# Graph attention with LayerNorm: k and q weights staged by column pieces, first scores after two projections, v's low parts on GpSimd

## The chip, the core and the metric

The kernel runs on one NeuronCore of a Trainium2 chip. A core has five engines with instruction streams of their own: TensorE (PE in the profile), VectorE (DVE), ScalarE (ACT), GpSimd (POOL) and SyncE (SP, used here for DMA issues only). They meet through semaphores. The metric is the device time of one execution in microseconds (us), as the median of several executions.

## The reference, cut to what matters

```python
# x: (128 graphs, 128 nodes, 512); adj: (128, 128, 128); 16 heads of 32
q = split_heads(x @ Wq.T)
k = split_heads(x @ Wk.T)
v = split_heads(x @ Wv.T)
bias = (adj + adj)[:, None]
a = jnp.einsum('bhnd,bhmd->bhnm', q, k) * scale + bias
row_nonzero = jnp.any(a != 0, axis=-1, keepdims=True)
a = jnp.where(row_nonzero, a, -jnp.inf)
p = jax.nn.softmax(a, axis=-1)
p = jnp.where(jnp.isnan(p), 0.0, p)
o = jnp.einsum('bhnm,bhmd->bhnd', p, v)
o = o.transpose(0, 2, 1, 3).reshape(B, N, D)
y = _layernorm(x + o @ Wo.T)
```

## The kernel before

Four graphs make a group (512 nodes), so there are 32 groups. The 512 channels are cut into 4 chunks of 128 for the contraction and 4 head tiles of 128 columns (4 heads) for the output. One phase is one head tile of one group: 128 phases. `scores(f)` makes the scores of phase f in PSUM. VectorE then adds the doubled adjacency and takes row maxima (`bias`, line 851), takes row minima (`smallest`, 859), forms row factors (`largest`, `any_nonzero`, `row_factors`, lines 866, 874, 891), scales the exponentials (`normalise`, 897) and turns them in blocks of 32 (`turn_blocks`, 907), in two halves of two graphs each. ScalarE makes the exponentials (`exps`, line 699) between the two, and copies every finished projection out of PSUM (`take`). SyncE carries the turned blocks through DRAM (`save_blocks`, `move_blocks`), and two phases later `values(f)` multiplies them with v.

A projection is called a product here: (kind, tile or graph, groups ahead). A product is done at fp32 precision as three matmuls of parts for each chunk, 12 matmuls of 128x512: every operand is split into a high part (a rounded copy, on ScalarE) and a low part (the rest, a subtraction of two SBUF tensors). The helper `rest` on VectorE is line 780, and on GpSimd line 349. Which products stand between two `scores` is written out by hand in `BEFORE`, `FIRST_PLAN` (group 0), `PLAN` and `LAST_PLAN`. The three PSUM banks of products are used in the order of these lists, and `take` follows them.

```python
FIRST_PLAN = [[("q", 1, 0), ("v", 0, 0), ("v", 1, 0), ("v", 2, 0)],
              [("k", 2, 0), ("q", 2, 0), ("v", 3, 0), ("v", 0, 1)],
              [("k", 3, 0), ("q", 3, 0), ("v", 1, 1)],
              [("k", 0, 1), ("q", 0, 1), ("v", 2, 1)]]
BEFORE = [("k", 0, 0), ("q", 0, 0), ("k", 1, 0)]
```

At the start, ScalarE's queue loads the k weights and SyncE's queue loads everything else, in chunks of 256 KB (128 partitions of 2 KB): xt of group 0, q, v, adjacency, xt of group 1, o. They land in tiles that the phases will use later (`w_stage`, `xt_stage`). VectorE makes the low parts of xt of group 0 and of k, q and v. GpSimd makes those of xt of group 1 and of o. Before phase f+1's `scores`, TensorE waits for ScalarE's copies of k and q (`k_copied`, `q_copied`) and for VectorE's `bias` of phase f.

The functions that the change touches, with the profile's line numbers:

Of the kernel before, what the change touches and what calls it, by code (L numbers as in the profile page):

```python
# [42 lines left out]
FIRST_PLAN = [[("q", 1, 0), ("v", 0, 0), ("v", 1, 0), ("v", 2, 0)],  # L43
# [7 lines left out]
BEFORE = [("k", 0, 0), ("q", 0, 0), ("k", 1, 0)]  # L51
# [60 lines left out]
def build(nc, xt_d, x_d, adj_d, wq_d, wk_d, wv_d, wo_d, out_d, blocks_d):  # L112
    ctx = ExitStack()
    with ctx:  # L114
# [6 lines left out]
        def sem(name):  # L121
# [101 lines left out]
        w_stage = {"k": v_sb[:, 1], "q": e_sb[:, :].rearrange("p a b c -> p a (b c)"),  # L223
                   "v": v_sb[:, 0], "o": x_sb[:, :, :]}
# [19 lines left out]
        def _(sp):  # L244
            def stage_w(kind, c):
                sp.dma_start(w_stage[kind][:, c], {"q": wq_d, "v": wv_d, "o": wo_d}[kind][:, c]
                             ).then_inc(w_loaded[kind, c], 16)

# [85 lines left out]
        def _(pool):  # L334
# [121 lines left out]
        def _(pe):  # L456
# [46 lines left out]
            def first_product(kind, index):  # L503
                def early(c):
                    pe.wait_ge(xt_hi_done, c + 1)
                    pe.wait_ge(w_hi_done, c + 1)

                def before(c):
                    if kind == "k":
                        pe.wait_ge(xt0_lo_done, c + 1)  # L510
                    n = CH * ORDER.index(kind) + c + 1
                    pe.wait_ge(w_hi_done, n)
                    pe.wait_ge(w_lo_done, n)
                weight_product(kind, 0, index, before if index == 0 else None, early if kind == "k" else None)
# [69 lines left out]
            for f in range(LAST):  # L584
# [3 lines left out]
                for kind, g, index in slots(f):  # L588
                    if g == 0 and kind == "v":
# [44 lines left out]
        def _(act):  # L634
# [107 lines left out]
            take(-1, 2)
            for f in range(PHASES):
# [3 lines left out]
                if f == 0:  # L747
                    act.wait_ge(w_lo_done, 2 * CH)
# [6 lines left out]
                if f == 0:  # L755
                    weight_hi("o")
# [21 lines left out]
        def _(dve):  # L778
# [3 lines left out]
            def weight_lo(kind, c):  # L782
                dve.wait_ge(w_hi_done, CH * ORDER.index(kind) + c + 1)
                w = WEIGHT[kind]
                rest(w_lo[:, w, c, :], w_stage[kind][:, c], w_hi[:, w, c, :]).then_inc(w_lo_done, 1)
# [131 lines left out]
            for c in range(CH):  # L917
                weight_lo("v", c)
# [73 lines left out]
```

## Time and profile before

| what | value |
|---|---|
| median of 3 executions | 1736.4 us (1736.4 to 1737.27) |
| profiled execution, its own time | 1735.29 us |
| its span in the profile | 1733.5 us |
| TensorE busy | 1708.4 us |
| VectorE busy | 1589.5 us |
| ScalarE busy | 1368.2 us |
| GpSimd busy | 962.1 us |

The profiled execution took 1735.29 us by its own time, 1.8 us of which lie outside the span. Its time is 1.1 us below the median of the three. The program has 128 phases, so one phase is some 13.3 us in the steady part.

### The profile page before, as it was taken

The numbers are of one execution on the slowest core, as the hardware profiler recorded it, in microseconds if no ns is written. First come the engines' busy times: TensorE is split into PE (matmuls) and PEld (weight loads), VectorE is DVE, ScalarE is ACT, GpSimd is POOL, SyncE is SP. The second block draws the span as 40 slices with busy tenths as digits, with TensorE's granted clock in tenths as the row PEclk, the third lists the DMA queues.
The fourth block names the chain that finished last, engine by engine and source line by source line (L and its number), as shares of the span: only waits on it lengthen the run. The fifth ranks groups of instructions, "written<-read, shape, count | busy, mean of one in ns | idle before, by whom it ended". The sixth has DMA issues, their size and how long they took to land. (4 is left out here: it accounts for less than half of the span.)

```text
span 1733.5 us, 45700 instructions
## 1 busy us (share of the span) xinstructions
PE 1708.4 (99%) x14370; PEld 1379.8 (80%) x14370; DVE 1589.5 (92%) x5815; ACT 1368.2 (79%) x5134; POOL 962.1 (55%) x1516
## 2 busy tenths in 40 slices
PE   9899999999999999999999999999999999999996
PEld 7788888888888888888888888788888888888884
DVE  7999999999999999999999999999999999999996
ACT  7787788788778877887788788778877887888775
POOL 2255556555555555565555555555655556556543
PEclk9999999999999999999999999999999999999999
DMA  6677777777777777777777777777777777777764
GB/s 213 199 225 216 226 225 227 223 216 230 226 220 225 232 218 226 214 233 224 215 231 228 223 229 215 223 225 224 234 220 216 225 225 227 226 211 234 211 200 168
DMA packets 275378, 382.59 MB, mean 221 GB/s; under 512 B 25152, under 2 KB 155200, under 8 KB 275008
## 3 DMA queue, kind: packets, MB, share of 16 engines
q1 hardware_dynamic: 274560, 378.64, 74.1%
q8 instruction: 113, 1.85, 0.5%
q14 instruction: 129, 1.06, 0.2%
q10 hardware_dynamic: 576, 1.05, 0.2%
HBM read 212.86 MB, written 166.72 MB: 219 GB/s over the span
## 5 line engine op out<-in xcount | busy, mean ns | idle before, releaser
L699 ACT ACTIVATE e_sb<-neg_a,neg_max 128x128 f32<-128x128 f32 x2048 | 793.2, 391 | 164.2 <-DVE neg_max L851 164.2
L851 DVE CUSTOM_DVE_ANT_0 neg_a<-ps_s,adj_sb 128x128 f32<-128x128 f32 x2048 | 442.4, 286 | 67.3 <-PE ps_s L536 67.1
L469 PE MATMUL ps_w<-xt_hi,w_lo 128*128 128x512 f32 x1020 | 414.4, 406 | 0.0
L470 PE MATMUL ps_w<-xt_lo,w_hi 128*128 128x512 f32 x1020 | 400.4, 393 | 0.0
L699 ACT ACTIVATION_READ_ACCUMULATOR e_sb<-neg_a,neg_max 128x1 f32 x2048 | 387.9, 189 | 0.0
L907 DVE STREAM_TRANSPOSE e_b<-e_sb 128x1024 f32<-128x1024 f32 x254 | 316.3, 1245 | 27.2 <-DVE e_sb L897 0.9
L349 POOL TENSOR_TENSOR o_lo<-o_sb,o_hi 128x512 fp32r<-128x512 f32 x126 | 163.8, 1300 | 289.7 <-ACT o_sb L636 289.7
L897 DVE SCALAR_TENSOR_TENSOR e_sb<-e_sb,r_inv 128x1024 f32<-128x1024 f32 x256 | 316.4, 1236 | 8.1 <-DVE r_inv L891 0.5
L859 DVE TENSOR_REDUCE neg_min<-neg_a 128x16 f32<-128x2048 f32 x128 | 292.6, 2286 | 4.4
L472 PE MATMUL ps_w<-xt_hi,w_hi 128*128 128x512 f32 x1020 | 274.0, 391 | 0.0
L469 PEld LDWEIGHTS ps_w<-xt_hi,w_lo 128*128 128x128 f32 x1020 | 191.3, 188 | 64.5 <-issue 25.3
L365 POOL TENSOR_TENSOR x_sb<-y_sb,x_sb 128x512 f32<-128x512 f32 x122 | 156.5, 1283 | 145.0 <-ACT y_sb L636 144.8
L472 PEld LDWEIGHTS ps_w<-xt_hi,w_hi 128*128 128x128 f32 x1020 | 191.7, 188 | 42.1
L470 PEld LDWEIGHTS ps_w<-xt_lo,w_hi 128*128 128x128 f32 x1020 | 191.9, 188 | 36.8
L636 ACT ACTIVATE y_sb<-ps_w 128x512 f32<-128x512 f32 x122 | 72.8, 597 | 165.7 <-PE ps_w L472 165.7
L469 PE MATMUL ps_w<-w_hi,xt_lo 128*128 128x512 f32 x512 | 199.4, 389 | 0.0
L470 PE MATMUL ps_w<-w_lo,xt_hi 128*128 128x512 f32 x512 | 199.3, 389 | 0.0
L469 PE MATMUL ps_w<-w_hi,o_lo 128*128 128x512 f32 x496 | 193.3, 390 | 0.0
L470 PE MATMUL ps_w<-w_lo,o_hi 128*128 128x512 f32 x496 | 193.1, 389 | 0.0
L851 DVE DVE_READ_ACCUMULATOR2_ANT neg_max<- 128x1 f32 x2048 | 170.5, 83 | 0.0
L536 PEld LDWEIGHTS ps_s<-k_sb,q_sb 32*128 32x128 f32 x4096 | 126.0, 186 | 52.2 <-issue 52.2
L349 POOL TENSOR_TENSOR xt_lo<-xt_raw,xt_hi 128x512 fp32r<-128x512 f32 x120 | 158.2, 1319 | 15.8 <-ACT xt_hi L636 15.8
(104 smaller groups left out, 2622.4 us busy)
## 6 DMA issues: line engine op xcount, KB each, us to landing
blocks<-e_b SPq DMA_DIRECT2D x1016, 128.0 KB, 2.2
e_t<-blocks SPq DMA_DIRECT2D x127, 1024.0 KB, 7.2
x_sb<-x SPq DMA_DIRECT2D x124, 256.0 KB, 4.8
out<-x_sb SPq DMA_DIRECT2D x124, 256.0 KB, 3.6
xt_raw<-xt SPq DMA_DIRECT2D x120, 256.0 KB, 4.8
adj_sb<-adj SPq DMA_DIRECT2D x32, 256.0 KB, 5.1
v_sb<-wk ACTq DMA_DIRECT2D x4, 256.0 KB, 6.4
neg_a<-xt SPq DMA_DIRECT2D x4, 256.0 KB, 5.9
```

Of the source, the lines that this page charges most:

```text
L349: return pool.tensor_tensor(out, whole, hi.bitcast(F32), ALU.subtract)
L365: pool.tensor_tensor(row, y_sb[:, :], row, ALU.add).then_inc(added, 1)
L469: pe.matmul(out, lhs_lo(c), rhs_hi(c), start=(c == 0), stop=False)
L470: pe.matmul(out, lhs_hi(c), rhs_lo(c), start=False, stop=False)
L472: last = pe.matmul(out, lhs_hi(c), rhs_hi(c), start=False, stop=(c == chunks - 1))
L536: last = pe.matmul(ps_s[h][:, nodes], q_sb[rows, slot, nodes], k_sb[rows, slot, nodes], start=True, stop=True)
L636: return act.activation(out, in_, ACT.Copy, scale=scale)
L699: last = act.activation(e_sb[:, i, h, :], neg_a[:, i, h, :], ACT.Exp, scale=-1.0, bias=neg_max[:, i, h:h + 1], accum_out=sums[:, i, h:h + 1])
L851: last = dve.tensor_tensor_reduce(out=neg_a[:, i, h, :], in0=ps_s[h][:, i * NODES:(i + 1) * NODES], in1=adj_sb[:, g % PAIR, i, :], scale=- ...
L859: dve.tensor_reduce(neg_min[:, :].rearrange("p a b -> p (a b)"), neg_a[:, :].rearrange("p a b c -> p (a b) c"), AX.X, ALU.max).then_inc(mi ...
L897: dve.scalar_tensor_tensor(out=e_sb[:, two].rearrange("p i h n -> p (i h) n"), in0=e_sb[:, two].rearrange("p i h n -> p (i h) n"), scalar=BIG,
L907: dve.transpose(blocks[:, half], e_sb[:, 2 * half:2 * half + 2].rearrange("p i h (b j) -> p (i h) b j", b=BLOCKS)).then_inc(transposed, 1)
```

## The change

The staged weights of k and q are cut by columns of the output instead of by chunks of the contraction. `PIECES` gives three pieces: the columns of head tile 0, those of head tile 1, and those of tiles 2 and 3 together. A piece holds all four chunks, so the first piece of k is all that the first product needs of k. The first pieces of k and q are loaded on ScalarE's queue, the other four on SyncE's. The high parts of the six pieces are on ScalarE. The low parts of the four narrow pieces are on VectorE, and those of the two wide ones on GpSimd (two instructions of 128x1024 elements). The low parts of v (four of 128x512) move from VectorE to GpSimd. q is staged in `x_sb` instead of `e_sb`, so ScalarE's wait before the first exponentials goes, and SyncE now waits for all pieces of k and q to be split before it loads o. The high parts of xt of group 1 move behind the exponentials of phase 0, those of o behind phase 1's.

```diff
-FIRST_PLAN = [[("q", 1, 0), ("v", 0, 0), ("v", 1, 0), ("v", 2, 0)],
-              [("k", 2, 0), ("q", 2, 0), ("v", 3, 0), ("v", 0, 1)],
-              [("k", 3, 0), ("q", 3, 0), ("v", 1, 1)],
+FIRST_PLAN = [[("k", 1, 0), ("q", 1, 0), ("v", 0, 0), ("v", 1, 0)],
+              [("k", 2, 0), ("q", 2, 0), ("v", 2, 0), ("v", 3, 0)],
+              [("k", 3, 0), ("q", 3, 0), ("v", 0, 1), ("v", 1, 1)],
-BEFORE = [("k", 0, 0), ("q", 0, 0), ("k", 1, 0)]
+BEFORE = [("k", 0, 0), ("q", 0, 0)]
+PIECES = [slice(0, P), slice(P, 2 * P), slice(2 * P, D)]
...
+            def stage_piece(kind, n):
+                cols = PIECES[n]
+                sp.dma_start(w_stage[kind][:, :, cols], {"k": wk_d, "q": wq_d}[kind][:, :, cols]
+                             ).then_inc(piece_loaded[kind, n], 16)
...
-            for c in range(CH):
-                stage_w("q", c)
+            stage_piece("k", 1)
+            stage_piece("q", 1)
             for c in range(CH):
                 stage_w("v", c)
             sp.dma_start(adj_sb[:, 0], adj_d[0]).then_inc(adj_loaded[0], 16)
+            stage_piece("k", 2)
+            stage_piece("q", 2)
             for c in range(CH):
                 stage_chunk(1, c)
+            sp.wait_ge(piece_hi_done, 6)
+            sp.wait_ge(piece_lo_done, 4)
+            sp.wait_ge(rest_lo_done, 2)
             for c in range(CH):
                 stage_w("o", c)
...
             for c in range(CH):
+                pool.wait_ge(wv_hi_done, c + 1)
+                rest(w_lo[:, WEIGHT["v"], c, :], w_stage["v"][:, c], w_hi[:, WEIGHT["v"], c, :]).then_inc(wv_lo_done, 1)
+            for kind in "kq":
+                w, cols = WEIGHT[kind], PIECES[2]
+                pool.wait_ge(piece_hi_done, 5 + "kq".index(kind))
+                rest(w_lo[:, w, :, cols], w_stage[kind][:, :, cols], w_hi[:, w, :, cols]).then_inc(rest_lo_done, 1)
...
+            def piece_hi(kind, n):
+                act.wait_ge(piece_loaded[kind, n], 16)
+                copy(w_hi[:, WEIGHT[kind], :, PIECES[n]], w_stage[kind][:, :, PIECES[n]]).then_inc(piece_hi_done, 1)
...
+            piece_hi("k", 0)
             for c in range(CH):
                 staged_hi(0, c)
-                act.wait_ge(w_loaded["k", c], 16)
-                copy(w_hi[:, WEIGHT["k"], c, :], w_stage["k"][:, c]).then_inc(w_hi_done, 1)
-            weight_hi("q")
+            piece_hi("q", 0)
             take(-1, 0)
+            piece_hi("k", 1)
+            piece_hi("q", 1)
+            take(-1, 1)
             weight_hi("v")
-            take(-1, 1)
-            for c in range(CH):
-                staged_hi(1, c)
-            take(-1, 2)
...
+                    if f == 0 and i == 1:
+                        piece_hi("k", 2)
+                        piece_hi("q", 2)
...
+            piece_lo("k", 0)
             for c in range(CH):
                 dve.wait_ge(xt_hi_done, c + 1)
                 rest(xt_lo[:, 0, c, :], xt_stage[0, c], xt_hi[:, 0, c, :]).then_inc(xt0_lo_done, 1)
-                weight_lo("k", c)
-            for c in range(CH):
-                weight_lo("q", c)
-            for c in range(CH):
-                weight_lo("v", c)
+            piece_lo("q", 0)
+            piece_lo("k", 1)
+            piece_lo("q", 1)
```

The first place is ScalarE at the start of the program, before. `v_sb` stages k here, `neg_a` stages xt of group 0.

```order
L731 DMA v_sb<-wk 128x512 x4
L636 ACT_TABLE_LOAD
L636 ACTIVATE xt_hi<-neg_a 128x512 [waits xt_staged00]
L636 ACTIVATE w_hi<-v_sb 128x512 [waits wk_loaded0]
L636 ACTIVATE xt_hi<-neg_a 128x512 [waits xt_staged01]
L636 ACTIVATE w_hi<-v_sb 128x512 [waits wk_loaded1]
```

The same place of the changed kernel, up to the copy of the first q product; `x_sb` stages q.

```order
L773 DMA v_sb<-wk 128x4x128
L773 DMA x_sb<-wq 128x4x128
L673 ACT_TABLE_LOAD
L673 ACTIVATE w_hi<-v_sb 128x4x128 [waits k_piece_loaded0]
L673 ACTIVATE xt_hi<-neg_a 128x512 [waits xt_staged00]
L673 ACTIVATE xt_hi<-neg_a 128x512 [waits xt_staged01]
L673 ACTIVATE xt_hi<-neg_a 128x512 [waits xt_staged02]
L673 ACTIVATE xt_hi<-neg_a 128x512 [waits xt_staged03]
L673 ACTIVATE w_hi<-x_sb 128x4x128 [waits q_piece_loaded0]
L673 ACTIVATE k_sb<-ps_w 128x512 [waits k_made]
L673 ACTIVATE w_hi<-v_sb 128x4x128 [waits k_piece_loaded1]
L673 ACTIVATE w_hi<-x_sb 128x4x128 [waits q_piece_loaded1]
```

Eight conversions and the four of q before the first copy out of PSUM have become six, and the one that all others stand behind waits for the first piece of k.

The second place is GpSimd from its first real work on, before.

```order
L349 TENSOR_TENSOR xt_lo<-e_t,xt_hi 128x512 [waits xt_hi_done,consts]
L349 TENSOR_TENSOR xt_lo<-e_t,xt_hi 128x512 [waits xt_hi_done] x3
L349 TENSOR_TENSOR w_lo<-x_sb,w_hi 128x512 [waits w_hi_done] x4
L349 TENSOR_TENSOR o_lo<-o_sb,o_hi 128x512 [waits values_copied]
L349 TENSOR_TENSOR xt_lo<-xt_raw,xt_hi 128x512 [waits xt_hi_done] x2
```

The same place of the changed kernel. The first two rows are v's, the next two k's and q's wide pieces, then xt of group 1 and o.

```order
L365 TENSOR_TENSOR w_lo<-v_sb,w_hi 128x512 [waits wv_hi_done,consts]
L365 TENSOR_TENSOR w_lo<-v_sb,w_hi 128x512 [waits wv_hi_done] x3
L365 TENSOR_TENSOR w_lo<-v_sb,w_hi 128x4x256 [waits piece_hi_done]
L365 TENSOR_TENSOR w_lo<-x_sb,w_hi 128x4x256 [waits piece_hi_done]
L365 TENSOR_TENSOR xt_lo<-e_t,xt_hi 128x512 [waits xt_hi_done] x4
L365 TENSOR_TENSOR w_lo<-x_sb,w_hi 128x512 [waits wo_hi_done] x4
L365 TENSOR_TENSOR o_lo<-o_sb,o_hi 128x512 [waits values_copied]
```

Six subtractions, two of them twice as wide, now stand ahead of the eight that were there.

The third place is ScalarE in phase 0, before.

```order
L699 ACTIVATE e_sb,sums<-neg_a,neg_max 128x128 [waits biased]
L699 ACTIVATE e_sb,sums<-neg_a,neg_max 128x128 x3
L636 ACTIVATE q_sb<-ps_w 128x512 [waits q_made]
L699 ACTIVATE e_sb,sums<-neg_a,neg_max 128x128 [waits biased]
L699 ACTIVATE e_sb,sums<-neg_a,neg_max 128x128 x3
```

The same place of the changed kernel, and on to the end of the phase.

```order
L673 ACTIVATE k_sb<-ps_w 128x512 [waits k_made]
L673 ACTIVATE w_hi<-v_sb 128x4x256 [waits k_piece_loaded2]
L673 ACTIVATE w_hi<-x_sb 128x4x256 [waits q_piece_loaded2]
L741 ACTIVATE e_sb,sums<-neg_a,neg_max 128x128 [waits biased]
L741 ACTIVATE e_sb,sums<-neg_a,neg_max 128x128 x3
L741 ACTIVATE e_sb,sums<-neg_a,neg_max 128x128 [waits biased]
L741 ACTIVATE e_sb,sums<-neg_a,neg_max 128x128 x3
L673 ACTIVATE q_sb<-ps_w 128x512 [waits q_made]
L673 ACTIVATE xt_hi<-e_t 128x512 [waits xt_staged10]
L673 ACTIVATE xt_hi<-e_t 128x512 [waits xt_staged11]
```

Between the exponentials of the phase's two halves stand two conversions of 128x1024, and the four of xt of group 1 come behind the second half.

## Rows read from the trace of the kernel before

**Rows 1.** The page, part 1: busy time (share of the span), instructions.

```profile
PE 1708.4 (99%) x14370; PEld 1379.8 (80%) x14370; DVE 1589.5 (92%) x5815; ACT 1368.2 (79%) x5134; POOL 962.1 (55%) x1516
```

**Rows 2.** Busy by stretch: stretch, us, busy of each engine (instructions), PEclk, DMA, GB/s.

```profile
140.00:200.00 60.00, 60.00 (x517) 48.56 (x519) 55.18 (x192) 47.21 (x178) 35.24 (x58) 1.00 0.76 225
200.00:1700.00 1500.00, 1496.18 (x12671) 1210.92 (x12663) 1392.12 (x5136) 1197.32 (x4521) 864.06 (x1352) 1.00 0.76 223
```

**Rows 3.** Waits of TensorE: line, waited for: us in total, times, longest.

```profile
PE ps_s L536 <- issue: 7.0, 5, 2.0
```

**Rows 4.** Timeline, TensorE, the scores (L536): start us, us, [idle before].

```profile
18.24 1.17 PE L536 MATMUL ps_s<-k_sb,q_sb 32*128 32x128 f32 x32
...
54.82 1.17 PE L536 MATMUL ps_s<-k_sb,q_sb 32*128 32x128 f32 x32 [1.56 <-issue]
...
66.97 1.17 PE L536 MATMUL ps_s<-k_sb,q_sb 32*128 32x128 f32 x32 [1.58 <-issue]
...
79.28 1.17 PE L536 MATMUL ps_s<-k_sb,q_sb 32*128 32x128 f32 x32 [1.75 <-issue]
...
92.50 1.17 PE L536 MATMUL ps_s<-k_sb,q_sb 32*128 32x128 f32 x32
```

**Rows 5.** Timeline, VectorE, the first bias instruction of phases 0 to 3.

```profile
19.59 0.29 DVE L851 CUSTOM_DVE_ANT_0 neg_a<-ps_s,adj_sb 128x128 f32<-128x128 f32 x1 [2.65 <-PE ps_s L536]
...
33.27 0.25 DVE L851 CUSTOM_DVE_ANT_0 neg_a<-ps_s,adj_sb 128x128 f32<-128x128 f32 x1
...
45.38 0.25 DVE L851 CUSTOM_DVE_ANT_0 neg_a<-ps_s,adj_sb 128x128 f32<-128x128 f32 x1
...
57.48 0.25 DVE L851 CUSTOM_DVE_ANT_0 neg_a<-ps_s,adj_sb 128x128 f32<-128x128 f32 x1
```

**Rows 6.** Timeline, VectorE, scaling and row factors of phase 0's two halves.

```profile
26.09 1.23 DVE L897 SCALAR_TENSOR_TENSOR e_sb<-e_sb,r_inv 128x1024 f32<-128x1024 f32 x1
...
28.72 1.06 DVE L891 SCALAR_TENSOR_TENSOR r_inv<-recip,nonzero 128x8 f32<-128x8 f32 x1
29.81 2.26 DVE L897 SCALAR_TENSOR_TENSOR e_sb<-e_sb,r_inv 128x1024 f32<-128x1024 f32 x1
```

**Rows 7.** Timeline, GpSimd, its two trains of subtractions in the first 40 us.

```profile
17.28 5.02 POOL L349 TENSOR_TENSOR xt_lo<-e_t,xt_hi 128x512 fp32r<-128x512 f32 x4 [15.51 <-ACT xt_hi L636]
28.46 6.03 POOL L349 TENSOR_TENSOR w_lo<-x_sb,w_hi 128x512 fp32r<-128x512 f32 x4 [6.15 <-ACT w_hi L636]
```

**Rows 8.** Timeline, ScalarE: first conversions, then phase 0's exponentials and copies.

```profile
5.12 0.63 ACT L636 ACTIVATE xt_hi<-neg_a 128x512 fp32r<-128x512 f32 x1 [1.22 <-DMA neg_a<-xt]
5.66 0.61 ACT L636 ACTIVATE w_hi<-v_sb 128x512 fp32r<-128x512 f32 x1
...
20.62 0.40 ACT L699 ACTIVATE e_sb<-neg_a,neg_max 128x128 f32<-128x128 f32 x1 [0.97 <-DVE neg_max L851]
...
23.72 0.57 ACT L636 ACTIVATE q_sb<-ps_w 128x512 f32<-128x512 f32 x1
...
27.28 0.57 ACT L636 ACTIVATE v_sb<-ps_w 128x512 f32<-128x512 f32 x1
```

**Rows 9.** Timeline, TensorE, product matmuls: the first ones, then two products' first.

```profile
6.42 0.77 PE L461 MATMUL ps_w<-xt_hi,w_hi 128*128 128x512 f32 x1 [0.39 <-ACT w_hi L636]
...
7.79 0.63 PE L464 MATMUL ps_w<-xt_lo,w_hi 128*128 128x512 f32 x1
8.21 0.63 PE L461 MATMUL ps_w<-xt_hi,w_hi 128*128 128x512 f32 x1
...
22.19 0.39 PE L469 MATMUL ps_w<-w_hi,xt_lo 128*128 128x512 f32 x1
...
24.91 0.39 PE L469 MATMUL ps_w<-w_hi,xt_lo 128*128 128x512 f32 x1
```

**Rows 10.** DMA queue 1 from 9.5 to 16 us: packets, MB, share of 16 engines.

```profile
q1 hardware_dynamic: 1383, 2.52, 105.5%
```

**Rows 11.** The same queue from 28.6 to 35 us.

```profile
q1 hardware_dynamic: 774, 0.71, 42.9%
```

More of the change, by code:

```diff
@@ L176, in build @@
         CONSTS = 11
-        w_loaded = {(kind, c): sem(f"w{kind}_loaded{c}") for kind in ORDER for c in range(CH)}
-        w_hi_done = sem("w_hi_done")
-        w_lo_done = sem("w_lo_done")
+        w_loaded = {(kind, c): sem(f"w{kind}_loaded{c}") for kind in "vo" for c in range(CH)}
+        piece_loaded = {(kind, n): sem(f"{kind}_piece_loaded{n}") for kind in "kq" for n in range(3)}
+        piece_hi_done = sem("piece_hi_done")
+        piece_lo_done = sem("piece_lo_done")
+        rest_lo_done = sem("rest_lo_done")
+        wv_hi_done = sem("wv_hi_done")
+        wv_lo_done = sem("wv_lo_done")
+        wo_hi_done = sem("wo_hi_done")
         wo_lo_done = sem("wo_lo_done")
@@ L436, in _ @@
             for c in range(CH):
+                pool.wait_ge(wv_hi_done, c + 1)
[4 more added lines that the diff above has]
+                rest(w_lo[:, w, :, cols], w_stage[kind][:, :, cols], w_hi[:, w, :, cols]).then_inc(rest_lo_done, 1)
+            for c in range(CH):
                 pool.wait_ge(xt_hi_done, CH + c + 1)
@@ L503, in first_product, with before @@
             def first_product(kind, index):
+                if kind == "v":
+                    def before(c):
+                        pe.wait_ge(wv_hi_done, c + 1)
+                        pe.wait_ge(wv_lo_done, c + 1)
+                    weight_product(kind, 0, index, before if index == 0 else None)
+                    return
                 def early(c):
                     pe.wait_ge(xt_hi_done, c + 1)
-                    pe.wait_ge(w_hi_done, c + 1)
                 def before(c):
[L509 to L514, printed above, removed]
+                    if c == 0:
+                        pe.wait_ge(piece_lo_done, 1)
+                    pe.wait_ge(xt0_lo_done, c + 1)
+                n = "kq".index(kind) + 1
+                pe.wait_ge(piece_hi_done, 2 * min(index, 2) + n)
+                if index > 1:
+                    pe.wait_ge(rest_lo_done, n)
+                elif index or kind == "q":
+                    pe.wait_ge(piece_lo_done, 2 * index + n)
+                if index == 0 and kind == "k":
+                    weight_product(kind, 0, index, before, early)
+                else:
+                    weight_product(kind, 0, index)
             def turn(i):
@@ L588, in _ @@
                 for kind, g, index in slots(f):
-                    if g == 0 and kind == "v":
+                    if g == 0 and kind != "o":
                         first_product(kind, index)
@@ L755, in _ @@
                 if f == 0:
+                    for c in range(CH):
+                        staged_hi(1, c)
+                elif f == 1:
                     weight_hi("o")
@@ L780, in rest, with piece_lo @@
                 return dve.tensor_tensor(out, whole, hi.bitcast(F32), ALU.subtract)
[L782 to L785, printed above, removed]
+            def piece_lo(kind, n):
+                w, cols = WEIGHT[kind], PIECES[n]
+                dve.wait_ge(piece_hi_done, 2 * n + "kq".index(kind) + 1)
+                rest(w_lo[:, w, :, cols], w_stage[kind][:, :, cols], w_hi[:, w, :, cols]).then_inc(piece_lo_done, 1)
             def double_adj(g):
@@ L913, in _ @@
                 rest(xt_lo[:, 0, c, :], xt_stage[0, c], xt_hi[:, 0, c, :]).then_inc(xt0_lo_done, 1)
-                weight_lo("k", c)
-            for c in range(CH):
-                weight_lo("q", c)
-            for c in range(CH):
-                weight_lo("v", c)
+            piece_lo("q", 0)
+            piece_lo("k", 1)
+            piece_lo("q", 1)
             double_adj(0)
```

20 lines of the change are left out of this document (10 added, 10 removed).

## The prediction

> **What bounds the kernel now.** I read the page's busy times first, then the stretches, then TensorE's waits and the places of its `scores`, then VectorE around them. TensorE is busy for 1708.4 of 1733.5 us [rows 1]. From 140 us on it is busy all of the time, 1496.18 of 1500 us in the long stretch [rows 2], and VectorE, at 1392.12 there, has room. The product count does not change, so the change can act only on what TensorE loses before about 80 us. There are two such losses. The first is the opening: the scores of phase 0 start at 18.24 [rows 4]. The second is three gaps, of 1.56, 1.58 and 1.75 us, 4.9 together, before the scores of phases 3, 4 and 5 at 54.82, 66.97 and 79.28 [rows 4]; they are most of the 7.0 us that TensorE waits at L536 in the whole run [rows 3]. At 92.50 there is no gap any more.
>
> Behind the gaps stands VectorE. Its softmax stages begin at 19.59, 33.27, 45.38 and 57.48 [rows 5], and none but the first has idle time ahead of it. A stage is 12.1 us long (33.27 to 45.38, 45.38 to 57.48), the first one 13.7. TensorE starts the scores of phase 3 at 54.82, 9.4 after stage 2 began at 45.38: they wait for q, which ScalarE copies only after that stage's exponentials. So up to 79.28 the start of VectorE's first stage and the lengths of its stages set the time. From there on TensorE is the bound, and a shift of the 79.28 stays to the end.
>
> Why is stage 0 longer by 1.6 us? Its second half shows a row factor instruction (128x8 elements) of 1.06 us and a scaling of 2.26, where the first half's scaling took 1.23 [rows 6]. Just then, from 28.46, GpSimd runs four subtractions in a row, 6.03 us instead of the 5.02 that its earlier four took [rows 7]. The row factor ends at 29.78, about when the first subtraction (28.46 + 1.25) ends, and the scaling then loses one more subtraction. So a VectorE instruction that reads two SBUF tensors waits for the GpSimd instruction under way, and in the gap between two VectorE instructions the next subtraction slips in. The bias instructions from 19.59, which read PSUM, ran beside the earlier train at their usual 0.29 us [rows 5, 7].
>
> **The change, part by part.**
>
> *Opening.* Now ScalarE starts at 5.12, TensorE at 6.42 [rows 8, 9]. New: everything on ScalarE stands behind the first piece of k. Its rows are 512 bytes. With 2 KB packets the queue used 105.5% of 16 engines over 6.5 us for 2.52 MB, 43.5 engine-us per MB [rows 10]; with mostly 1 KB packets 42.9% over 6.4 us for 0.71 MB, 62 per MB [rows 11]. The trace has no 512-byte packets. Least: no dearer per byte, and the piece lands by 5.1. Most: each costs as much as a 1 KB packet (0.063 us) and alternates with a 2 KB packet (0.089 us) of the other queue, 32 of each per engine, 4.9 us against 1.4 now, so 3.4 later. Between them I continue the trend, a factor of 1.4 per halving, which makes a piece 1.4 us of pure transfer instead of 0.7, and take a landing at 6.0. Two conversions (0.54 apart, as 5.12 and 5.66) and a hand-over of 0.15 (6.27 to 6.42) put the first matmul at 7.3.
>
> The profile's clock column shows full clock from its first record, but the spacing of matmuls shows the lower level at first: 0.42 us from 7.79 to 8.21, against 2.72 us for twelve, 0.23 each, from 22.19 to 24.91 [rows 9]; that is 1.2 against 2.4 GHz. It rose near 11.2. I let it rise at the same time. Then the first product ends near 12.1, hardly earlier than now, for twelve matmuls at 0.42 take 5 us whatever feeds them. The q product, which now waits for VectorE's low parts, has them all ready and takes 2.7 instead of 3.3: it ends at 14.8. The k1 product that stood next hid ScalarE's copy of q. Without that cover the copy costs 0.57 [rows 8] and two hand-overs, about 0.8: scores at 15.6. VectorE's first stage follows 1.35 later (18.24 to 19.59), at 17.0. **Term 1: −2.6 us** (16.3 to 19.5 for the two ends of the transfer, the later one taking the clock's rise with it: −3.3 to −0.1).
>
> *Stage 0 of VectorE.* I count from its start. ScalarE ends the first half's exponentials at 4.1 (23.72 − 19.59, [rows 8]), copies k1 until 4.6, then converts the two wide pieces. A copy of 512 is 0.54 in a row; one of 1024 lies between that and 1.08, I take 1.0. The pieces are ready at 5.7 and 6.7, the second half's exponentials at 9.7, xt of group 1 from 10.9. GpSimd is done with v by then: its four start before stage 0, beside bias instructions only. It goes through the wide pieces from 5.8. A subtraction of 512 takes 1.25 (5.02 / 4); one of 1024 between 1.25 and 2.5, I take 2.3, near the double, since time follows elements. VectorE's small instructions for the first half start at about 5.8 to 6.3 and its scaling at 6.5 (26.09 − 19.59). The row factor waits until 8.1. The second wide one slips in, so the scaling waits until 10.4 and ends at 11.7. The second half's row factor comes 1.4 after that (27.32 to 28.72) and meets xt's train of four; it and the scaling lose about one subtraction each, as in rows 6. The scaling ends near 16.9, and the next stage starts 1.2 later (32.07 to 33.27), at 18.1. Moving the lengths within their bounds gives 17.7 to 19.8, as one more subtraction slips in or not. I take 18.2 against 13.7. **Term 2: +4.5 us** (+4.0 to +6.1). ScalarE's added 2 us is hidden in it.
>
> *Stage 1.* The train for o moves here, behind ScalarE's conversions at the same place in the stage as in stage 0 before, and costs the 1.6 us seen there. **Term 3: +1.6 us.**
>
> *At no cost.* v's low parts leave VectorE while it would idle (2.65 us ahead of 19.59, [rows 5]). v's first product comes 6.5 us after the scores' start, and GpSimd's last of v is ready some 1 us sooner; without that the lateness would fall on TensorE, which has slack in this stretch. SyncE's queue: o's four loads and the adjacency wait for the second wide piece, at about 10.4 of stage 0. Behind them stands `save_blocks` of the first half, itself not ready before 13. The fourth product in phase 2 costs TensorE 2.7 us, but it then has 4 to 8 us in hand, since VectorE is late: from 15.6 its own work would bring it to the scores of phase 5 at 15.6 + (79.28 − 18.24 − 4.9) + 2.7 = 74.5. A gap of some 4 us before the scores of phase 2 may lower its clock; the next phase has about 2 us of slack for it.
>
> *Sum.* −2.6 + 4.5 + 1.6 = +3.5: scores of phase 5 at 82.8 instead of 79.28. On the profiled execution's 1735.29 that is 1738.8, and on the median of 1736.4 (1.1 above it) **1740 us**.
>
> One rule of the Trainium skill (SBUF — State Buffer, "SBUF: two separate sides") would make term 2 larger. It says that the port pair shared by VectorE and GpSimd is an exclusive lock held for a whole instruction, and that VectorE wants it also for one-input instructions in a two-port mode. By it `any_nonzero` (L874, one input) waits for the first wide piece as well and the second slips in ahead of the row factor; the sum would be nearer +5 than +3.5. No row of before has that instruction beside a subtraction.
>
> Another speaks for the change: by DMA: Bandwidth & Descriptors, "Specifications", line rate needs transfers of 512 bytes or more. By it the pieces would be at full rate, and term 1 would be −3.3. Rows 10 and 11 disagree: packets above that size already differ by a factor of 1.4.
>
> **The rivals.** The forecast has 0.55, with its own range of 1738 to 1743.
>
> *Faster: GpSimd's longer trains cost VectorE no more than the one did before* (0.17). That is so if VectorE gets the port back before the next subtraction: in rows 6 it did not, twice. Then stages 0 and 1 are 13.7 and 12.1 and only term 1 stands: 1733.8. If nothing at all blocks, TensorE's own floor of 74.5 decides: 1731.6. It decides from where terms 2 and 3 together fall below 2.6.
>
> *Cancelled: no change to measure* (0.13). Stage 0 loses only about one subtraction more than before, for instance because the wide pieces are quicker, near the lower bound of 1.25: 2.6 lost against 2.6 gained, 1736.4.
>
> *The first piece is late* (0.15). The two queues alternate packet by packet, term 1 is −0.1, the rest stands: 1742.5.
>
> **How the numbers follow.** A measurement of this kernel tells about 0.2% (3.5 us) from no change, 1732.9 to 1739.9. The forecast lies at the edge: of its 0.55, 0.36 are above 1739.9 and 0.19 below. The late piece is slower. Of the faster case 0.09 lie under 1732.9 and 0.08 above. So faster 0.09, same 0.08 + 0.13 + 0.19 = 0.40, slower 0.36 + 0.15 = 0.51. The range for 8 in 10 leaves out the deepest of the faster case and the extreme of the late one: 1733.5 to 1743.
>
> **What would show it.** The first stage of VectorE near 17.0 and the second 18.2 after it; in it a row factor instruction of about 2 us, a scaling of over 3, and GpSimd's two 128x1024 subtractions beside them; 13.7 to the third stage; a TensorE gap of about 4 us before the scores of phase 2 and further ones up to phase 5, whose scores start near 82.8. The prediction is wrong if stage 0 is near 13.7, if scores of phase 5 come before 79.28, or if a piece costs the opening more than it saves.

## The result, and the profile after

The changed kernel takes 1741.22 us (median of 10 executions, 1739.56 to 1742.6), the kernel before 1737.05 (median of 10). The ratio is 1.0025, with a 95% interval of 1.0015 to 1.0035: 4.2 us slower, where 3.6 had been forecast. The profiled execution took 1742.6 us, 1.4 above its median; the likely reason lies in its last 40 us, below.

The busy times of the engines, from the page of the changed kernel. TensorE does the same work as in [rows 1] within 2 us, on a span that is 7.3 us longer.

```profile
PE 1710.4 (98%) x14370; PEld 1382.0 (79%) x14370; DVE 1592.7 (91%) x5807; ACT 1367.8 (79%) x5132; POOL 974.1 (56%) x1522
```

The timeline of TensorE in the changed kernel, its scores (L573) and what waited ahead of them: start us, us, what, [idle before].

```profile
15.38 1.17 PE L573 MATMUL ps_s<-k_sb,q_sb 32*128 32x128 f32 x32 [0.78 <-ACT q_sb L673]
...
40.49 0.50 PE L492 MATMUL ps_w<-w_hi,xt_lo 128*128 128x512 f32 x1 [3.35 <-ACT k_sb L673]
...
45.03 1.17 PE L573 MATMUL ps_s<-k_sb,q_sb 32*128 32x128 f32 x32
...
59.19 1.17 PE L573 MATMUL ps_s<-k_sb,q_sb 32*128 32x128 f32 x32
...
71.05 1.17 PE L573 MATMUL ps_s<-k_sb,q_sb 32*128 32x128 f32 x32 [1.26 <-issue]
...
83.36 1.17 PE L573 MATMUL ps_s<-k_sb,q_sb 32*128 32x128 f32 x32 [1.70 <-issue]
```

The first scores come 2.9 us earlier than in [rows 4] (15.38 against 18.24), and pay 0.78 for the copy of q. By the scores of phase 5 the kernel is 4.1 us late (83.36 against 79.28), and this stays: its last scores start 4.7 us late (1699.47 against 1694.77), the 0.6 more from a wait just behind the scores of phase 5 (0.63 us at 85.17, for the move of the turned blocks). In between TensorE stood still for 3.35 us, ahead of v's product 3, whose bank was freed by ScalarE's late copy of k2.

VectorE's stages in the changed kernel, from its timeline: the first bias instruction (L896) of phases 0 to 3.

```profile
16.71 0.29 DVE L896 CUSTOM_DVE_ANT_0 neg_a<-ps_s,adj_sb 128x128 f32<-128x128 f32 x1 [2.04 <-PE ps_s L573]
...
35.72 0.25 DVE L896 CUSTOM_DVE_ANT_0 neg_a<-ps_s,adj_sb 128x128 f32<-128x128 f32 x1
...
49.45 0.25 DVE L896 CUSTOM_DVE_ANT_0 neg_a<-ps_s,adj_sb 128x128 f32<-128x128 f32 x1
...
61.55 0.25 DVE L896 CUSTOM_DVE_ANT_0 neg_a<-ps_s,adj_sb 128x128 f32<-128x128 f32 x1
```

Beside [rows 5]: stage 0 is 19.0 us instead of 13.7, stage 1 13.7 instead of 12.1, stage 2 12.1 as before. So −2.88 + 5.33 + 1.62 = +4.07 us, with 16.71 − 19.59 as the first term and the growth of stages 0 and 1 as the others. The next group shows where stage 0 lost its time: VectorE in it, without the bias instructions.

```profile
22.42 0.19 DVE L927 RECIPROCAL recip<-sums 128x8 f32<-128x8 f32 x1
22.54 2.29 DVE L911 SCALAR_TENSOR_TENSOR abs_max<-neg_max,neg_min 128x16 f32<-128x16 f32 x1
24.86 2.32 DVE L919 TENSOR_SCALAR nonzero<-abs_max 128x16 f32<-128x16 f32 x1
27.29 0.17 DVE L936 SCALAR_TENSOR_TENSOR r_inv<-recip,nonzero 128x8 f32<-128x8 f32 x1
27.49 2.29 DVE L942 SCALAR_TENSOR_TENSOR e_sb<-e_sb,r_inv 128x1024 f32<-128x1024 f32 x1
...
31.18 1.03 DVE L936 SCALAR_TENSOR_TENSOR r_inv<-recip,nonzero 128x8 f32<-128x8 f32 x1
32.24 2.27 DVE L942 SCALAR_TENSOR_TENSOR e_sb<-e_sb,r_inv 128x1024 f32<-128x1024 f32 x1
```

And GpSimd's timeline over the same time.

```profile
15.90 5.05 POOL L365 TENSOR_TENSOR w_lo<-v_sb,w_hi 128x512 fp32r<-128x512 f32 x4 [14.13 <-ACT w_hi L673]
22.39 2.41 POOL L365 TENSOR_TENSOR w_lo<-v_sb,w_hi 128x1024 fp32r<-128x1024 f32 x1 [1.44 <-ACT w_hi L673]
24.75 2.41 POOL L365 TENSOR_TENSOR w_lo<-x_sb,w_hi 128x1024 fp32r<-128x1024 f32 x1
27.42 6.01 POOL L365 TENSOR_TENSOR xt_lo<-e_t,xt_hi 128x512 fp32r<-128x512 f32 x4 [0.26 <-ACT xt_hi L673]
```

The two lists fit together. `abs_max` has 16 elements a row and takes 2.29 us, until GpSimd's first wide subtraction ends at 24.80. `nonzero` (the instruction of `any_nonzero`) takes 2.32, until the second ends at 27.16. The row factor at 27.29, between two trains, takes its usual 0.17. The first scaling takes 2.29 instead of 1.23, behind xt's first, and the second half meets xt's train as in [rows 6]. The reciprocal at 22.42, with the wide subtraction under way since 22.39, took its usual 0.19.

The opening: ScalarE's first conversion waits for the first piece of k, which lands shortly before 5.46, and the first matmul follows at 6.75.

```profile
5.46 0.63 ACT L673 ACTIVATE w_hi<-v_sb 128x512 fp32r<-128x512 f32 x1 [2.09 <-DMA v_sb<-wk]
```

The price of small packets in the changed kernel: DMA queue 1 from 7.9 to 8.7 us, mostly 512-byte packets, and then from 13.2 to 14.4, 1 KB packets: packets, MB, share of 16 engines.

```profile
q1 hardware_dynamic: 402, 0.26, 119.0%
```

```profile
q1 hardware_dynamic: 424, 0.42, 110.8%
```

That is 59 engine-us per MB for the first (119.0% of 16 over 0.8 us) and 51 for the second, against 43.5 for 2 KB in [rows 10]. The window of the first is short and also holds some 2 KB packets. Queue 10 carries nothing but the first pieces of k and q, all in 512-byte packets, and gives 54 over its whole load (from 0 to 10 us).

```profile
q10 hardware_dynamic: 1056, 0.52, 17.5%
```

So a byte in 512-byte packets costs 1.24 to 1.35 times what it costs in 2 KB packets. The 62 of [rows 11], which had stood in for 1 KB, were mostly writes to DRAM.

In this execution 3.2 of the 7.3 us of span come after the scores of phase 5, 2.6 of them after the last scores. There TensorE waits until 1703.5 for a move of the turned blocks, 2.88 us, and starts again slowly (1.68 us for what takes 1.08).

```profile
1703.52 1.68 PE L593 MATMUL ps_o<-e_t,v_sb 128*32 128x128 f32 x32 [2.88 <-DMA e_t<-blocks]
```

The kernel before had waits of 0.5 and 0.8 us at these places. The medians differ by 4.2 us, close to the shift already there at phase 5, so I count the rest of this wait as the spread of single executions; that is argued from the medians and not shown by a second profile.

### The profile page after: what moved, and what is told of

It reads as the page before. It is cut to its first block and busy times, and to the rows that moved or that the text cites. A ratio compares the mean times of both kernels' runs of the same rounds, so it can differ in the third digit from the quotient of the medians.

```text
span 1740.8 us, 45691 instructions
## 1 busy us (share of the span) xinstructions
PE 1710.4 (98%) x14370; PEld 1382.0 (79%) x14370; DVE 1592.7 (91%) x5807; ACT 1367.8 (79%) x5132; POOL 974.1 (56%) x1522
## 5 line engine op out<-in xcount | busy, mean ns | idle before, releaser
L896 DVE CUSTOM_DVE_ANT_0 neg_a<-ps_s,adj_sb 128x128 f32<-128x128 f32 x2048 | 442.6, 287 | 66.0 <-PE ps_s L573 65.9
L741 ACT ACTIVATION_READ_ACCUMULATOR e_sb<-neg_a,neg_max 128x1 f32 x2048 | 392.3, 192 | 0.0
L896 DVE DVE_READ_ACCUMULATOR2_ANT neg_max<- 128x1 f32 x2048 | 172.1, 84 | 0.0
L573 PEld LDWEIGHTS ps_s<-k_sb,q_sb 32*128 32x128 f32 x4096 | 126.0, 186 | 49.9 <-issue 49.9
```

The source lines that it names most:

```text
L573: last = pe.matmul(ps_s[h][:, nodes], q_sb[rows, slot, nodes], k_sb[rows, slot, nodes], start=True, stop=True)
L741: last = act.activation(e_sb[:, i, h, :], neg_a[:, i, h, :], ACT.Exp, scale=-1.0, bias=neg_max[:, i, h:h + 1], accum_out=sums[:, i, h:h + 1])
L896: last = dve.tensor_tensor_reduce(out=neg_a[:, i, h, :], in0=ps_s[h][:, i * NODES:(i + 1) * NODES], in1=adj_sb[:, g % PAIR, i, :], scale=- ...
```

## The experiments

Seven kernels, each timed in five rounds beside the kernel before, in two groups that share their runs of it (medians 1737.34 and 1737.32). "First stage" is the start of VectorE's first stage, "stage 0" to "stage 2" are the lengths of its stages, and "phase 5" is the start of the scores of phase 5, all in us and from one profiled execution of each kernel.

| kernel | first stage | stage 0 | stage 1 | stage 2 | phase 5 | median us | ratio to before (95%) |
|---|---|---|---|---|---|---|---|
| before | 19.59 | 13.7 | 12.1 | 12.1 | 79.28 | 1737.3 | |
| changed | 16.71 | 19.0 | 13.7 | 12.1 | 83.36 | 1741.2 | 1.0025 (1.0015 to 1.0035) |
| e1, wide low parts on VectorE | 16.71 | 15.5 | 13.8 | 12.6 | 80.46 | 1738.9 | 1.0006 (0.9997 to 1.0015) |
| e2, k1 before the scores | 19.18 | 18.0 | 13.7 | 12.1 | 84.84 | 1743.7 | 1.0033 (1.0022 to 1.0045) |
| e3, order only | 17.78 | 12.8 | 12.1 | 12.7 | 77.22 | 1735.4 | 0.9988 (0.998 to 0.9997) |
| e5, two extra subtractions | 19.76 | 17.7 | 12.1 | 12.1 | 83.43 | 1741.0 | 1.0023 (1.0015 to 1.0032) |
| e4, trains in the free stretch | 16.90 | 16.0 | 12.1 | 14.3 | 81.12 | 1737.2 | 1.0002 (0.9994 to 1.0011) |
| e6, pieces without contention | 17.80 | 12.2 | 12.2 | 13.3 | 77.27 | 1734.2 | 0.9984 (0.9975 to 0.9993) |
| e7, order and one wait | 17.63 | 12.1 | 12.2 | 13.3 | 77.06 | 1735.4 | 0.9992 (0.9983 to 1.0001) |

The median less the start of phase 5 is 1656.1 to 1658.9 us in all nine, while that start moves over 7.8 us. So what the opening loses stays, to within some 2 us: single executions also differ behind phase 5, and e4, at the low end, has the same median as the kernel before although its phase 5 comes 1.8 us later.

**e5, the contention alone, put into the kernel before.**

```diff
+            pool.wait_ge(exp_done, 2)
+            for n in range(2):
+                rest(o_lo[:, 2 * n:2 * n + 2, :], w_hi[:, WEIGHT["q"], 0:2, :].bitcast(F32),
+                     w_hi[:, WEIGHT["k"], 0:2, :]).then_inc(extra_done, 1)
+            pool.wait_ge(extra_done, 2)
             for c in range(CH):
                 pool.wait_ge(w_hi_done, 3 * CH + c + 1)
```

> The kernel before, with two extra subtractions of 128x1024 on GpSimd in stage 0, from the end of the first half's exponentials on; what they write is overwritten later, and nothing waits for them but GpSimd. My theory: the contention alone makes VectorE's stage 0 long; it goes from 13.7 to near 17.9 us, with abs_max, any_nonzero or the row factor at about 2 us instead of 0.17, and the time rises by 4.2 to 1741.2 us. Rival, that GpSimd's work is hidden and the stage was lengthened by something else of the change: stage 0 stays at 13.7 and the time at 1737.

Measured: stage 0 of 17.7 us and 1741.0 us. Nothing of the change is in this kernel but GpSimd's two wide instructions at that place, and stage 0 grows by 4.0 us. That its time equals the changed kernel's is a coincidence of sums: the changed one gains 2.9 in the opening, and loses 5.3 in stage 0 and 1.6 in stage 1. VectorE's timeline in e5:

```profile
25.59 0.92 DVE L872 SCALAR_TENSOR_TENSOR abs_max<-neg_max,neg_min 128x16 f32<-128x16 f32 x1
26.54 2.33 DVE L880 TENSOR_SCALAR nonzero<-abs_max 128x16 f32<-128x16 f32 x1
28.97 1.26 DVE L897 SCALAR_TENSOR_TENSOR r_inv<-recip,nonzero 128x8 f32<-128x8 f32 x1
30.27 2.26 DVE L903 SCALAR_TENSOR_TENSOR e_sb<-e_sb,r_inv 128x1024 f32<-128x1024 f32 x1
```

GpSimd's timeline in e5 has the two from 24.07, and o's train right behind them.

```profile
24.07 4.77 POOL L350 TENSOR_TENSOR o_lo<-w_hi 128x1024 fp32r<-128x1024 f32 x2 [1.76 <-ACT e_sb L705]
28.91 4.77 POOL L350 TENSOR_TENSOR w_lo<-x_sb,w_hi 128x512 fp32r<-128x512 f32 x3
```

Each small instruction ends when one of GpSimd's does, and four in a row meet a new one. The rival, that GpSimd's work is hidden, falls.

**e1, the same contention taken out of the changed kernel.**

```diff
-            for kind in "kq":
-                w, cols = WEIGHT[kind], PIECES[2]
-                pool.wait_ge(piece_hi_done, 5 + "kq".index(kind))
-                rest(w_lo[:, w, :, cols], w_stage[kind][:, :, cols], w_hi[:, w, :, cols]).then_inc(rest_lo_done, 1)
...
                 smallest(f)
+                if f == 0:
+                    for kind in "kq":
+                        w, cols = WEIGHT[kind], PIECES[2]
+                        dve.wait_ge(piece_hi_done, 5 + "kq".index(kind))
+                        rest(w_lo[:, w, :, cols], w_stage[kind][:, :, cols], w_hi[:, w, :, cols]
+                             ).then_inc(rest_lo_done, 1)
```

> The changed kernel, with the two wide low parts taken from GpSimd and made on VectorE right behind the row minima of stage 0. My theory: VectorE's stage 0 was 19.0 us because it waited for GpSimd's 128x1024 subtractions. Doing them itself costs VectorE 2.3 us, and only xt's train then meets its second half: stage 0 near 16.1 us, scores of phase 5 near 80.5 instead of 83.4, time 1738.3 us (2.9 below the changed kernel). Rival, that ScalarE's two wide conversions between the halves made the stage long: they are still there, so stage 0 would stay at 19 or rise by 2.3 to 21.3, time 1741 to 1743.5.

Measured: stage 0 of 15.5 us, phase 5 at 80.46, 1738.9 us. VectorE's timeline in e1 shows the work that it took over, and the small instructions at their usual length; only the second half still meets xt's train.

```profile
22.41 1.22 DVE L821 TENSOR_TENSOR w_lo<-v_sb,w_hi 128x1024 fp32r<-128x1024 f32 x1
23.54 1.22 DVE L821 TENSOR_TENSOR w_lo<-x_sb,w_hi 128x1024 fp32r<-128x1024 f32 x1
...
24.79 0.12 DVE L907 SCALAR_TENSOR_TENSOR abs_max<-neg_max,neg_min 128x16 f32<-128x16 f32 x1
24.95 0.18 DVE L915 TENSOR_SCALAR nonzero<-abs_max 128x16 f32<-128x16 f32 x1
...
28.75 2.27 DVE L938 SCALAR_TENSOR_TENSOR e_sb<-e_sb,r_inv 128x1024 f32<-128x1024 f32 x1
```

VectorE does in 2.3 us what cost it 4.3 of waiting when GpSimd did it (`abs_max` and `nonzero` fill 4.75 us up to the row factor, from 22.54 to 27.29, and 0.48 in the kernel before). ScalarE's wide conversions are still between the halves, so they were not the cause. Stage 2 is 12.6 us here because TensorE is late with phase 3's scores, as in e4 below.

**e2 and e3, the order of products by itself, from both sides.** e2 puts k1's product back ahead of the first scores of the changed kernel; e3 gives the kernel before the new order and nothing else; the rest of group 0 is dealt as in the change.

```diff
-BEFORE = [("k", 0, 0), ("q", 0, 0)]
+BEFORE = [("k", 0, 0), ("q", 0, 0), ("k", 1, 0)]
-FIRST_PLAN = [[("k", 1, 0), ("q", 1, 0), ("v", 0, 0), ("v", 1, 0)],
+FIRST_PLAN = [[("q", 1, 0), ("v", 0, 0), ("v", 1, 0)],
...
             take(-1, 1)
+            take(-1, 2)
             weight_hi("v")
```

> The changed kernel, with the k1 product put back ahead of the first scores (three products, then phase 0). My theory: the opening's gain is mostly from the order: the scores of phase 0 move from 15.4 to 17.3 (2.7 us of product, less the 0.8 of exposed copy), stage 0 keeps its 19 us, and all is 1.9 us later: 1743.1 us. Rival, that the time is set by TensorE's work and not by VectorE's first stage: the product is only moved, and the time stays at 1741.2 or falls by 0.8.

The edit of e3, on the kernel before:

```diff
-BEFORE = [("k", 0, 0), ("q", 0, 0), ("k", 1, 0)]
+BEFORE = [("k", 0, 0), ("q", 0, 0)]
-FIRST_PLAN = [[("q", 1, 0), ("v", 0, 0), ("v", 1, 0), ("v", 2, 0)],
+FIRST_PLAN = [[("k", 1, 0), ("q", 1, 0), ("v", 0, 0), ("v", 1, 0)],
...
-            take(-1, 2)
```

> The kernel before, with only the new order of products (two before the first scores, group 0 dealt anew), weights loaded and split as before. My theory: the scores of phase 0 start at 16.3 instead of 18.24, VectorE's first stage at 17.7, stage 0 stays near 13.7 and stage 1 at 12.1, so the scores of phase 5 come at 77.4 and the time is 1.9 us below the kernel before: 1735.2 us. Rival, that the new deal (a fourth product in phase 2) or the exposed copy of q itself costs time: no gain, 1737 us or above.

Measured: e2 starts its first scores at 17.84 and takes 1743.7 us, e3 at 16.45 and 1735.4. The order is worth 2.5 us of the opening in the changed kernel (17.84 − 15.38) and 1.8 in the one before (18.24 − 16.45). The pieces are worth 0.4 without the order (18.24 − 17.84) and 1.1 with it (16.45 − 15.38). The two pairs differ by single executions more than by the kernels: e2's second product starts at 12.28 and the changed kernel's at 11.69, with the same loads and the same work ahead of it. Less these 0.6 us, the order is worth 1.9 there too, which is what had been expected.

e2's stage 0 is 18.0 us, where 19 was expected. VectorE's timeline in e2 shows another set of instructions held.

```profile
25.01 0.17 DVE L912 SCALAR_TENSOR_TENSOR abs_max<-neg_max,neg_min 128x16 f32<-128x16 f32 x1
25.22 2.43 DVE L920 TENSOR_SCALAR nonzero<-abs_max 128x16 f32<-128x16 f32 x1
27.75 2.23 DVE L937 SCALAR_TENSOR_TENSOR r_inv<-recip,nonzero 128x8 f32<-128x8 f32 x1
30.02 1.22 DVE L943 SCALAR_TENSOR_TENSOR e_sb<-e_sb,r_inv 128x1024 f32<-128x1024 f32 x1
```

GpSimd's first wide subtraction starts at 25.21 here, 0.2 us after `abs_max`, which therefore passes; `nonzero` and the row factor wait for the two wide ones, and the scaling runs free, since xt's train starts only at 30.25. In e3 stage 0 is 12.8 us instead of 13.7, because o's train starts at 26.95, behind the start of the second half's row factor at 26.92; only the scaling waits (2.21 us). A shift of 0.2 us between the engines decides whether one more instruction waits.

The order alone, without the pieces and GpSimd's new work, makes the kernel 0.1% faster. Both rivals fall: moving a product that TensorE must do anyway changes the time, because VectorE starts sooner. e3's gain is small: 0.03 to 0.2% by its interval.

**e4, the trains moved to where VectorE does not wait for them.** The changed kernel with two waits on GpSimd, before xt's and before o's train.

```diff
+            pool.wait_ge(normalised, 2)
             for c in range(CH):
                 pool.wait_ge(xt_hi_done, CH + c + 1)
...
+            pool.wait_ge(normalised, 4)
             for c in range(CH):
                 pool.wait_ge(wo_hi_done, c + 1)
```

> The changed kernel, with two waits added on GpSimd: xt's train starts after VectorE's last scaling of stage 0, o's train after that of stage 1, so that both run beside bias and row minima, which do not wait for GpSimd. My theory: the wide pieces still cost stage 0 about 3.9 us, but the second half no longer waits: stage 0 near 16.0 us instead of 19.0, stage 1 12.1 instead of 13.7, scores of phase 5 near 78.8, time 1736.6 us, 4.6 below the changed kernel. Rival, that GpSimd's later low parts then hold TensorE up (the v product of group 1 or the move of the blocks waits for them): stages as said, but gaps before values or products in phase 2 and a time of 1739 to 1741.

Measured: stages 0 and 1 of 16.0 and 12.1 us as expected, and 1737.2 us, 4.0 below the changed kernel. VectorE's timeline in e4 keeps the waits for the wide pieces and loses the others.

```profile
22.72 2.28 DVE L913 SCALAR_TENSOR_TENSOR abs_max<-neg_max,neg_min 128x16 f32<-128x16 f32 x1
25.04 2.32 DVE L921 TENSOR_SCALAR nonzero<-abs_max 128x16 f32<-128x16 f32 x1
...
27.66 1.22 DVE L944 SCALAR_TENSOR_TENSOR e_sb<-e_sb,r_inv 128x1024 f32<-128x1024 f32 x1
...
30.48 1.22 DVE L944 SCALAR_TENSOR_TENSOR e_sb<-e_sb,r_inv 128x1024 f32<-128x1024 f32 x1
```

But phase 5 comes at 81.12 and not at 78.8: stage 2 takes 14.3 us. TensorE's timeline in e4 shows why.

```profile
41.33 1.17 PE L575 MATMUL ps_s<-k_sb,q_sb 32*128 32x128 f32 x32 [0.60 <-issue]
44.32 1.08 PE L595 MATMUL ps_o<-e_t,v_sb 128*32 128x128 f32 x32 [1.82 <-ACT v_sb L675]
...
58.04 1.17 PE L575 MATMUL ps_s<-k_sb,q_sb 32*128 32x128 f32 x32
```

Phase 2 has four products now, and with scores and values that is 13.3 us of TensorE. To these come 1.82 us of waiting for v's copies, which stand behind ScalarE's conversions of o, and about 1.7 us for eight matmuls at the lower clock behind this wait. The stretch from 44 to 49 us of e4 (columns as in [rows 2]) has a mean clock of 0.66.

```profile
44.00:49.00 5.00, 4.68 (x41) 3.71 (x42) 4.96 (x34) 3.23 (x13) 4.97 (x5) 0.66 0.78 208
```

The rival had GpSimd's lateness hold TensorE up; no such wait shows. It was ScalarE's, and TensorE's own work. The added waits did not bring it about: e1, which has none of them, has the same 1.82 us ahead of the same values, at 43.64, and phase 2 takes 16.7 us of TensorE in both.

**e6 and e7, versions without the contention.** e6 keeps the pieces: the wide ones are loaded ahead of v and split before the first stage, on VectorE. Their splitting is taken out where it stood, and GpSimd has e4's two waits; the cut below leaves both out. e7 is e3 with one wait.

```diff
             stage_piece("q", 1)
+            stage_piece("k", 2)
+            stage_piece("q", 2)
+            sp.dma_start(adj_sb[:, 0], adj_d[0]).then_inc(adj_loaded[0], 16)
             for c in range(CH):
                 stage_w("v", c)
-            sp.dma_start(adj_sb[:, 0], adj_d[0]).then_inc(adj_loaded[0], 16)
-            stage_piece("k", 2)
-            stage_piece("q", 2)
...
             piece_hi("q", 0)
-            take(-1, 0)
             piece_hi("k", 1)
             piece_hi("q", 1)
+            piece_hi("k", 2)
+            take(-1, 0)
+            piece_hi("q", 2)
             take(-1, 1)
...
             piece_lo("q", 1)
+            for kind in "kq":
+                w, cols = WEIGHT[kind], PIECES[2]
+                dve.wait_ge(piece_hi_done, 5 + "kq".index(kind))
+                rest(w_lo[:, w, :, cols], w_stage[kind][:, :, cols], w_hi[:, w, :, cols]).then_inc(rest_lo_done, 1)
```

> The changed kernel with the two waits of the run before, and the wide pieces of k and q loaded ahead of v and split before the first stage, their low parts on VectorE, in its idle time there; only v, xt of group 1 and o stay on GpSimd. My theory: VectorE's first stage still begins at 16.7, every stage is 12.1 us long, so VectorE allows the scores of phase 5 at 74.9 and TensorE's own work at 74.4: 4.4 us below the kernel before, 1732.8 us. Rival, that v's later landing or the conversions delay the opening: first stage at 17.5 or later, 1734 us or more.

The edit of e7, on e3:

```diff
+            pool.wait_ge(normalised, 2)
             for c in range(CH):
                 pool.wait_ge(w_hi_done, 3 * CH + c + 1)
```

> The kernel before with the new order of products (as the run of the order alone) and one wait on GpSimd, o's train after VectorE's last scaling of stage 0; no pieces. My theory: first stage at 17.8, every stage 12.1 us, scores of phase 5 near 76.0, 3.3 us below the kernel before: 1734.0 us. Rival, that the contention in stage 0 was hidden there by the slack of the new deal: the time of the order alone, 1735.4 us.

Measured: e6 1734.2 us, 0.16% below the kernel before; e7 1735.4. Stage 0 is 12.1 or 12.2 us in both, the length of a stage that waits for nobody. In e6 the opening is 1.1 us later than in the changed kernel, and its rival holds by both of its numbers (first stage at 17.80, 1734.2 us). ScalarE's timeline in e6 shows the reason: the wide pieces' conversions stand ahead of the copies of k and q, and the first of them waits 0.86 us for its piece to land, until 13.33. From there to the copy of q at 15.74 ScalarE has no idle time.

```profile
13.33 1.06 ACT L671 ACTIVATE w_hi<-v_sb 128x1024 fp32r<-128x1024 f32 x1 [0.86 <-DMA v_sb<-wk]
...
14.78 1.06 ACT L671 ACTIVATE w_hi<-x_sb 128x1024 fp32r<-128x1024 f32 x1
15.74 0.58 ACT L671 ACTIVATE q_sb<-ps_w 128x512 f32<-128x512 f32 x1
```

The third chunk of xt also came late in this execution (ScalarE waits 1.69 us for it, until 8.94), but that is over before 13.33, and q's product, whose last four matmuls take from 13.94 to 15.01, is done before ScalarE gets to its copy.

In both, phase 2 takes 13.3 us of TensorE's own work, so VectorE's stage 2 is 13.3 long. This also takes the gain of e7 over e3: its wait shortens stage 0 from 12.8 to 12.1, phase 5 comes 0.2 us sooner, and the medians are the same. e7's rival, the time of the order alone, came out. Between e6 and e7 the medians differ by 1.3 us, which no row of the opening explains, and their intervals overlap.

## Why the prediction was right

**The bound.** VectorE's first start and the lengths of its stages set the time up to phase 5, and the shift there stays. Against the kernel before, the scores of phase 5 move by −2.1, +1.2, +5.6 and +4.2 us in e3, e1, e2 and e5, and the medians by −2.0, +1.6, +6.4 and +3.6. The other three fit less well: +1.8, −2.0 and −2.2 at phase 5 in e4, e6 and e7, and −0.1, −3.2 and −1.9 in the medians. So the mechanism is shown, and a microsecond or two of a single median is not explained by it.

**The sum.** Forecast −2.6 + 4.5 + 1.6, measured −2.9 + 5.3 + 1.6: the two misses have opposite signs, so the total (+3.5 forecast, +4.1 at phase 5) is a little nearer than its largest term.

**Term 1, −2.6, measured −2.9.** The piece was ready at 5.46 and not at 6.0, so the rival of a late first piece falls. I had priced 512-byte packets from writes to DRAM, at twice the engine time per byte; they cost 1.24 to 1.35 times that of 2 KB packets (54 to 59 against 43.5 per MB). The Trainium skill's rule on line rate from 512 bytes (DMA: Bandwidth & Descriptors, "Specifications") was nearer than my factor here, and still not met. The first product ended near 11.9, where 12.1 was estimated, for the matmuls ran at the lower clock until about 10.9. The exposed copy of q cost 0.78 where 0.8 was forecast.

**Term 2, +4.5, measured +5.3.** The cause was right, GpSimd's wide subtractions holding VectorE's instructions, and the size was low by 0.8; which instructions would be held was partly wrong. The step that was short is "VectorE's small instructions for the first half start at about 5.8 to 6.3": I let `abs_max` and `any_nonzero` pass and stopped the row factor and the scaling. In the trace `abs_max` waits for the first wide subtraction; it reads two SBUF tensors, so my own rule held it as soon as the subtraction started first (22.39 against 22.54). `any_nonzero`, with one input, waits for the second, and the scaling then meets xt's train too. Of the signs named, the row factor of about 2 us and the scaling of over 3 did not come in the changed kernel (0.17 and 2.29). That `any_nonzero` waits is what the Trainium skill's rule on the shared port pair (SBUF — State Buffer, "SBUF: two separate sides") had said; four profiles (changed, e5, e4, e2) show it, at 2.32, 2.33, 2.32 and 2.43 us. The sum that I had put beside it, "nearer +5", was too high: +4.1 at phase 5, +4.2 in the medians. The wide subtraction took 2.41 against 2.3 assumed.

**Term 3, +1.6, measured +1.6.** Stage 1 is 13.7 us, and 12.1 with o's train moved (e4). The rivals in which the longer trains cost nothing more, or just cancel the gain, fall with terms 2 and 3.

**A slip in the rivals.** "If nothing at all blocks, TensorE's own floor of 74.5 decides" does not follow from the prediction's own rows: a first stage at 17.0 and stages of 12.1 put the scores of phase 5 at 75.1 (17.0 + 79.28 − 19.59 − 1.6), above that floor. The chances rest little on it. e6 and e7, with nothing blocked, reach phase 5 at 77.27 and 77.06, because phase 2 then costs TensorE 13.3 us.

**At no cost.** v's low parts on GpSimd did not show anywhere, and neither did SyncE's queue. The fourth product in phase 2 cost nothing in the changed kernel only because VectorE was late; with the contention gone it costs 1.2 us (12.1 to 13.3, e6 and e7). The "gap of some 4 us before the scores of phase 2" was there in size and not in place: 3.35 us ahead of phase 1's last product, for a PSUM bank, and 0.89 ahead of the values. The clock fell as suspected; from 38 to 45 us its mean was 0.76.

```profile
38.00:45.00 7.00, 4.51 (x12) 3.12 (x12) 6.59 (x20) 7.00 (x32) 0.41 (x1) 0.76 0.68 216
```

It used up the slack: the scores at 59.19 follow TensorE's last product directly, 0.3 us after VectorE's 49.45 + 9.44 would have let them.

**Open.** Whether the wide piece in e6 lands as late as 13.33 in other executions was not settled; up to 1.1 us of its opening hang on it. That `any_nonzero` waits because of its input and output being both in SBUF was not tested by itself.

## What to carry to other kernels

Work moved from VectorE to GpSimd is not off VectorE: here a short VectorE instruction with two SBUF inputs, and a `tensor_scalar` with one, could wait for a whole GpSimd subtraction (up to 2.4 us), so place GpSimd's trains beside VectorE work that they do not stop (here bias and row minima, 5.8 of 12.1 us), and keep single instructions short. Read which engine sets the pace in the stretch that is edited, not in the whole run: TensorE is 99% busy here, and yet VectorE decided the first 80 us. When two gains are bound together with a cost, run each alone: the order by itself gave −0.1%, the whole change +0.25%.

## What the runs showed of the hardware

- A VectorE `tensor_scalar` of 16 elements with one input in SBUF waited 2.3 us for a GpSimd subtraction, like those with two inputs; a reciprocal of 8 elements beside the same subtraction took its usual 0.19, and bias (0.29), row minima (2.29) and the turning of blocks (1.25) kept their usual lengths beside GpSimd's trains.
- When a GpSimd subtraction ends and another follows, the next VectorE instruction, 0.03 us behind the last, meets the new one and waits again; four VectorE instructions in a row waited in e5 (0.92, 2.33, 1.26 and 2.26 us). One that started 0.2 us ahead of the subtraction was not held (`abs_max` in e2, 0.17 us).
- Loads cost 43.5, 51 and 54 to 59 engine-us per MB with packets of 2 KB, 1 KB and 512 bytes.
- Gaps of 3.35 (changed) and 1.82 us (e1, e4) in TensorE's work were followed by matmuls of 128x512 that started 0.43 us apart instead of 0.23, the level of 1.2 instead of 2.4 GHz; gaps of 1.56, 1.58 and 1.75 us in the kernel before were not. Between them it went both ways: gaps of 1.74 and 0.35 us (e1, ahead of 80.46 and 81.99) and of 1.75 and 0.54 (e2, ahead of 84.84 and 86.56) were followed by the lower level, gaps of 1.70 and 0.63 (changed, ahead of 83.36 and 85.17) were not. In e1 and e2 this put about 2 us between the scores of phases 5 and 6 that the kernel before does not have.
